# Two 16-head attentions of 32 entries each run as one sequence of 64 entries in one block

## The reference, cut to what matters

```
x = x + L0_xattn(ctx, layernorm(x), ...)        # 8 heads
x = x + L0_ffn(layernorm(x), ...)               # router picks 512 of 1536 units, up to 3 rounds
x = x + L1_xattn(layernorm(x), ctx, ctx, causal mask, w_q, w_k, w_v, w_o)   # 16 heads of 8, 120 keys
y = layernorm(x)
y = y + mla(rmsnorm(y) * g1, Wq, Wdkv, Wuk, Wuv, Wo)  # 16 heads of 8, 128 keys, causal
y = y + moe(rmsnorm(y) * g2, ...)               # 8 experts, top 2
x = x + y

# both attentions, per entry and head:
scores = q @ k.T / sqrt(8), masked;  a = softmax(scores);  out = (a @ v) @ wo
```

## Time and profile before

| | before |
|---|---|
| median of 3 runs | 1343.3 us |
| the profiled execution's own time | 1344.71 us |
| its span | 1342.9 us |
| granted TensorE clock, mean | 0.964 of full |
| busy: TensorE / VectorE / ScalarE / GpSimd | 1228.8 / 927.4 / 798.7 / 590.4 us |
| l1 pipeline | about 597 to 845 us of the span |
| mla pipeline | about 850 to 1086 us of the span |

### The profile page before, as it was taken

The page is one execution under the profiler, slowest core; times in us unless marked ns, Lnnn a source line. Parts: engine busy times, 40 slices in busy tenths (PEclk is TensorE's granted clock), DMA queues, the critical chain, the costliest instruction groups (busy, mean ns, idle before and its releaser), DMA issues. The chain is left out here.

```text
span 1342.9 us, 37984 instructions
## 1 busy us (share of the span) xinstructions
PE 1228.8 (92%) x13719; PEld 879.0 (65%) x13719; DVE 927.4 (69%) x1995; ACT 798.7 (59%) x2101; POOL 590.4 (44%) x677
## 2 busy tenths in 40 slices
PE   1799999999999995969999999599999979999996
PEld 0466666666666663437777777488888847777775
DVE  6476776776776773757989989399999956333431
ACT  0578778778778862216777777266666633333332
POOL 3587566566566555013233232543333224333343
PEclk9899999999999997988999999599999979999998
DMA  8000000000000000000000000200000000000000
GB/s 210 17 1 1 0 0 0 0 0 0 0 0 0 0 1 1 0 6 10 10 7 11 10 7 6 64 3 0 0 0 0 2 1 9 9 8 8 8 10 16
DMA packets 22740, 14.71 MB, mean 11 GB/s; under 512 B 6378, under 2 KB 21610, under 8 KB 22540
## 3 DMA queue, kind: packets, MB, share of 16 engines
q1 hardware_dynamic: 22520, 13.75, 3.9%
q10 hardware_dynamic: 148, 0.01, 0.0%
HBM read 11.66 MB, written 2.10 MB: 10 GB/s over the span
## 5 line engine op out<-in xcount | busy, mean ns | idle before, releaser
L694 POOL TENSOR_TENSOR r_norm<-ssm,mhalf 128x24 f32<-128x24 f32 x32 | 134.9, 4214 | 161.5 <-DVE ssm L599 161.5
L1938 ACT ACTIVATE moe_hid<-psum 128x512 f32<-128x512 f32 x128 | 76.4, 598 | 137.9 <-PE psum L1872 137.9
L537 ACT ACTIVATE l_probs<-psum,l_n_max 128x248 f32<-128x248 f32 x256 | 117.2, 481 | 57.5 <-DVE l_n_max L617 57.5
L2096 POOL TENSOR_TENSOR moe_acc<-moe_acc,moe_prod 128x512 f32<-128x512 f32 x64 | 81.3, 1271 | 147.8 <-DVE moe_prod L2052 147.8
L1882 PEld LDWEIGHTS psum<-w,moe_hid 128*128 128x128 f32 x1024 | 123.1, 192 | 27.0 <-issue 27.0
L2052 DVE TENSOR_TENSOR moe_prod<-psum,moe_combine 128x512 f32<-128x512 f32 x64 | 44.3, 692 | 136.2 <-PE psum L1882 136.1
L1882 PE MATMUL psum<-w,moe_hid 128*128 128x128 f32 x1024 | 123.4, 275 | 0.0
L1872 PE MATMUL psum<-moe_moe_hT,w 128*128 128x512 f32 x256 | 122.9, 608 | 0.0
L1726 POOL TENSOR_TENSOR mla_QX<-mla_qT,own_slots 128x512 f32<-128x512 f32 x32 | 33.3, 1042 | 136.0 <-ACT mla_qT L1560 136.0
L701 POOL TENSOR_TENSOR qkn<-qk,r_norm 128x1536 f32<-128x1536 f32 x32 | 88.4, 2762 | 2.5
L1726 POOL TENSOR_TENSOR l_QX<-l_qT,own_slots 128x512 f32<-128x512 f32 x32 | 33.3, 1042 | 122.3 <-ACT l_qT L1560 122.3
(11 more groups left out here) (311 smaller groups left out, 3393.2 us busy)
## 6 DMA issues: line engine op xcount, KB each, us to landing
X<-x_in SPq DMA_DIRECT2D x8, 256.0 KB, 4.9
out_dram<-moe_acc SPq DMA_DIRECT2D x32, 64.0 KB, 1.5
CT<-ctx_in SPq DMA_DIRECT2D x8, 240.0 KB, 6.1
l_cT<-ctxT_in SPq DMA_DIRECT2D x32, 60.0 KB, 1.8
w<-w_in SPq DMA_DIRECT2D x1, 1024.0 KB, 5.0
wm<-wm_in SPq DMA_DIRECT2D x1, 768.0 KB, 4.5
wp<-wp_in SPq DMA_DIRECT2D x1, 768.0 KB, 6.6
wkv<-wkv_in SPq DMA_DIRECT2D x1, 512.0 KB, 5.7
```

What stands on the lines that cost most here:

```text
L537: e = act.activation(probs[u][:, h, :], psum[:, 2 * u + h // 2, (h % 2) * K:(h % 2 + 1) * K], ACT.Exp, bias=n_max[u][:, h:h + 1], accum_ou ...
L694: pool.tensor_tensor(r_norm[:, :], ssm[:, :], mhalf[:, 0:3 * H], ALU.pow).then_inc(s["norm_inverted"], 1)
L1938: act.activation(hid[i % RING][:, :], psum[:, 2 + i % BANKS, :], ACT.Silu).then_inc(activated[i], 1)
L2096: pool.tensor_tensor(a[:, :, :], a[:, :, :], prod[e % 2][:, :, :], ALU.add).then_inc(summed[e], 1)
```

## The change

`attention16` becomes `attentions16`, which is called once. Its second block runs steps n from -2 to 65 over a sequence of 64 entries: entries 0 to 31 are l1's, entries 32 to 63 are mla's entries 0 to 31 (`is_l1`, `of_entry`, `row`). The steps inside are in the same order on each engine; a loop's body says by `l1` to which half it belongs. Steps 18 and 19 and steps 30 to 37 are among those written out.

The second attention's moments, taken of all 32 entries between the blocks before, are now taken by VectorE within the sequence: behind step 17 for entries 0 to 11 (`CHANGE = 12`), behind step 34 for entries 12 to 31. GpSimd takes the inverse roots at the end of steps 18 and 19 (12 columns each) and of steps 34, 35, 36 and 37 (10 columns each). `kT` and `probs` have room for 128 keys in both halves, of which l1 uses 120, so that l1's eight rows of 120 are no longer adjacent. SyncE's block is one: first the 32 loads of `cT`, then the expert weights.

```
-def moments(dve, stats6, mean, small, step):
+def moments(dve, stats6, mean, small, step, some=slice(0, B), base=0):
...
+def run_pair_steps(eng, body):
     for n in range(-2, 4):
         body(n, n % 2, n // 2)
     with eng.Fori(0, ROUNDS - 2) as i:
...
-    for n in range(2 * ROUNDS, 2 * ROUNDS + 2):
+    for n in range(2 * ROUNDS, 2 * ROUNDS + 4):
         body(n, n % 2, n // 2)
     with eng.Fori(0, B // 2 - 3 - ROUNDS) as i:
...
-    for n in range(B - 4, B + 2):
+    for n in range(B - 2, B + 6):
         body(n, n % 2, n // 2)
+    with eng.Fori(0, B // 2 - 4) as i:
+        body(2 * i + B + 6, 0, None, False)
+        body(2 * i + B + 7, 1, None, False)
+    for n in range(PAIR - 2, PAIR + 2):
+        body(n, n % 2, None)
...
-        probs = [sb(f"probs{i}", [P, H, K]) for i in range(2)]
+        probs = [sb(f"probs{i}", [P, H, P]) for i in range(2)]
...
+                def mla_moments(some, base):
+                    dve.wait_ge(x_stats, some.stop)
+                    moments(dve, stats6, mla_mean, small, step, some, base)
+                    dve.tensor_scalar(small[:, 0, some], small[:, 3, some], LN_EPS, None, ALU.add).then_inc(var_ready, 1)
+                    dve.tensor_scalar(small[:, 1, some], small[:, 3, some], 1.0 + RMS_EPS, RMS_EPS * LN_EPS, ALU.mult,
+                                      ALU.add).then_inc(var_ready, 1)
...
+                    if isinstance(n, int) and n == 2 * ROUNDS + 1:
+                        mla_moments(slice(0, CHANGE), 6)
+                    if isinstance(n, int) and n == B + 2:
+                        mla_moments(slice(CHANGE, B), 12)
...
+                def mla_scales(n):
+                    half = CHANGE + (B - CHANGE) // 2
+                    for at, some, ready in ((2 * ROUNDS + 2, slice(0, CHANGE), 3), (B + 2, slice(CHANGE, half), 5), (B + 4, slice(half, B), 5)):
+                        if isinstance(n, int) and n == at:
+                            pool.wait_ge(var_ready, ready)
+                            inverse_roots(pool, mla_rstd, small[:, 0, :], mhalf, some).then_inc(mla_scales_made, 1)
+                        if isinstance(n, int) and n == at + 1:
+                            inverse_roots(pool, mla_scale, small[:, 1, :], mhalf, some).then_inc(mla_scales_made, 1)
+                    if isinstance(n, int) and n in (B - 2, PAIR - 2):
+                        pool.wait_ge(mla_scales_made, 2 if n < B else 6)
...
+                def body(n, par, k, l1=None):
+                    centre(n + 1, l1)
+                    norm_output(n + 1, l1)
+                    norm_input(n + 1, l1)
                     spread_q(n + 1, 1 - par)
-                    if router and par == 0:
+                    if router and par == 0 and k is not None:
                         next_trials(k - 1)
                     later_scales(n)
+                    mla_scales(n)
```

More of the change, by code:

```diff
@@ L1312, in attention16 @@
         with nc.Block() as block:
-            if joined_from:
+            if router:
                 @block.tensor
@@ L1401, in attention16 @@
         scales_made = sem("scales_made")
+        mla_scales_made = sem("mla_scales_made")
         qkv_proj = sem("qkv_proj")
@@ L1430, in attention16, with there, is_l1, of_entry @@
         below4_made = sem("below4_made")
-        def row(T, n):
-            return T[:, entries(n), :].rearrange("p a d -> p (a d)")
+        def there(m):
+            return not isinstance(m, int) or 0 <= m < PAIR
+        def is_l1(m, l1):
+            return m < B if isinstance(m, int) else l1
+        def of_entry(T, m, l1):
+            return T[:, entries(m if is_l1(m, l1) else m - B)]
+        def row(T, m, l1):
+            return T[:, entries(m if is_l1(m, l1) else m - B), :].rearrange("p a d -> p (a d)")
+        def keys(m, l1):
+            return C if is_l1(m, l1) else P
         def round_there(k):
             return router and (not isinstance(k, int) or 0 <= k < 2 * ROUNDS)
-        def copy_input(eng, m):
+        def copy_input(eng, m, l1):
             if there(m):
@@ L1687, in body @@
                         wait(dve, totalled, k)
                     invert_sums(n - 1)
-                    if router and par == 0:
+                    if router and par == 0 and k is not None:
                         read_digit(k - 1)
                     scale_out(n - 1)
-                    max_a(n + 1, 1 - par)
+                    max_a(n + 1, 1 - par, l1)
                     if router and par == 0 and isinstance(k, int) and k == ROUNDS:
                         second_half()
-                steps(dve, body)
@@ L1710, in norm_input, with norm_output @@
                     if there(m):
+                        l1 = is_l1(m, l1)
                         wait(pool, x_centred, m + 1)
                         wait(pool, z_turned, m)
-                        pool.tensor_tensor(zn[:, :], centred[:, :], (rstd if l1 else scale)[:, entries(m)].broadcast_to([P, D]),
+                        pool.tensor_tensor(zn[:, :], centred[:, :], of_entry(rstd if l1 else mla_scale, m, l1).broadcast_to([P, D]),
                                            ALU.mult).then_inc(z_made, 1)
-                def norm_output(m):
-                    if there(m) and not l1:
+                def norm_output(m, l1):
+                    if there(m) and not is_l1(m, l1):
@@ L1757, in body @@
+                def body(n, par, k, l1=None):
+                    centre(n + 1, l1)
+                    norm_output(n + 1, l1)
+                    norm_input(n + 1, l1)
                     spread_q(n + 1, 1 - par)
-                    if router and par == 0:
+                    if router and par == 0 and k is not None:
                         next_trials(k - 1)
                     later_scales(n)
-                steps(pool, body)
-            if moe_weights:
-                @block.sync
-                def _(sp):
+                    mla_scales(n)
@@ new lines, in _, with load @@
+                run_pair_steps(pool, body)
+            @block.sync
+            def _(sp):
+                def load(m, par):
+                    wait(sp, qkv_proj, m - 1)
+                    sp.dma_start(cT[par][:, :], ctxT_in[entries(m)].rearrange("a d t -> (a d) t")).then_inc(c_loaded[par], 16)
+                load(0, 0)
+                load(1, 1)
+                with sp.Fori(0, B // 2 - 1) as i:
+                    load(2 * i + 2, 0)
+                    load(2 * i + 3, 1)
+                if moe_weights:
```

255 lines of the change are left out of this document (122 added, 133 removed).

## The result

Before 1343.91 us (median of 4 runs, 1341.84 to 1346.9), after 1333.89 us (4 runs, 1332.74 to 1335.86); ratio 0.9925, 95% interval 0.9913 to 0.9938, so 0.75% or 10.0 us less, clear of noise. The forecast was 1332.4 us, range 1328 to 1340. The profiled execution after took 1335.86 us with a span of 1333.7, so it is the slowest of its four; between the two profiled executions the span shrank by 9.2 us.

What follows compares the result with a forecast made beforehand. TensorE and VectorE were taken as full in mla's steady stretch, leaving the seam between the attentions to gain from: 22.7 us less 11.8 of costs is 10.9, from the median 1343.3 to 1332.4 us, range 1328 to 1340.

Steps and rivals of the forecast that it cites:

- seam, entries 31 to 35: Between l1 and mla: four entries' scores take 29.1 us instead of 51.8, a gain of 22.7 us.
- first moments, step 17: VectorE behind step 17: eight small rows cost 1.0 us, ends 0.3 and 1.3.
- root in step 18: GpSimd, 12 columns before entry 20's `centre`: TensorE already waits for `zn`, so its turn slips 2.3 us.
- root in step 19: GpSimd, 12 columns: 2.64 us of cover for 2.27, so cost 0; 2.3 if the cover is gone.
- wait and root in step 34: GpSimd waits for VectorE's second moments, then takes 10 columns: TensorE stands 5.0 us, ends 3.7 and 5.5.
- clock behind it: TensorE after step 35's idle: 4 to 7 us at half clock, cost 2.5 us, ends 0 and 3.5.
- roots in steps 35 to 37: GpSimd, 10 columns each: 1.96 us against 1.62 of cover, 0.34 each, 1.0 us in all.
- the clock at step 19: At step 19's start, where TensorE stands 2.3 + 0.55 us: no clock loss, 0, upper end 3.5 us.
- R1: Both stalls stay but the clock doesn't fall: net gain 13.4 us, 1330 us; chance 0.16.
- R2: Thin covers at steps 19 and 35 to 37, clock falls at both stalls: 1345 us, halfway 1339; chance 0.15.
- R3: l1's non-adjacent `probs` rows of 120 slow VectorE's shift and ScalarE's second exponential: 32 us exposed, 1364 us; chance 0.05.
- R4: Step 34's wait is not met, GpSimd being behind anyway: 0.34 us, no clock fall, net 18, 1325 us; chance 0.04.

Runs made afterwards that it cites:

- e4: Changed kernel without the in-sequence moments and roots (mean 0, scales 1 set once), a bound and no replacement: 1321.41 us, ratio 0.9836.
- e6: Changed kernel with throwaway transposes on TensorE, 24 ahead of entry 20's turn and 42 ahead of entry 36's: 1329.69 us, ratio 0.9895.
- e2: Changed kernel with the two first 12-column roots at the ends of steps 19 and 21 instead of 18 and 19: 1329.55 us, ratio 0.9892.
- e1: Changed kernel with the second moments behind VectorE's step 33 instead of step 34: 1327.82 us, ratio 0.9884.
- e3: Changed kernel with moments behind steps 18 and 33, roots at steps 19, 21 and 34 to 39 (6 or 7 columns in the last six): 1322.89 us, ratio 0.9844.
- e5: Changed kernel with CHANGE = 6 instead of 12, so first moments and roots cover 6 entries, the second 26: 1331.71 us, ratio 0.9910.

## Why the prediction was right, point by point

| term | predicted | measured in the traces |
|---|---|---|
| seam, entries 31 to 35 | 51.8 - 29.1 = 22.7 | 51.81 - 29.25 = 22.56; alone (e4) 22.0 in medians |
| first moments, step 17 | 1.0 | 0.83 (interval 7.84 against 7.01) |
| root in step 18 | 2.3, clock 0 | 4.74 = 1.97 idle (9.52 in e6 - 7.55) + 2.77 half clock |
| root in step 19 | 0 | 0.02 |
| wait and root in step 34 | 5.0 | 4.92 (e6: 11.67 - 6.75) |
| clock behind it | 2.5 | 2.47 (14.14 - 11.67) |
| roots in steps 35 to 37 | 1.0 | 0.76 over intervals of 6.75 |
| sum of costs | 11.8 | 13.7 |

- The mechanism held as it was told: the seam's gain, the queue order on GpSimd that turns a wait into TensorE's stall, the covers of 2.6 and 1.6 us, and that the clock falls at the stall of step 34. The costs of 13.7 leave 8.8 of the 9.2 us; the kernel before had itself an interval of 7.11 us before its mla entry 5, which the base of 6.75 does not count, and that is the 0.4.
- Single steps of l1 were read as 7.29 and 7.06 us, though their sum, 14.35, is not the pair of 14.51: in the loops they are 7.50 and 7.01. It did little harm. The seam's four intervals were 7.72, 7.07, 7.71 and 6.75, predicted 7.65, 7.06, 7.65 and 6.75. The root's own 2.3 was better than the table shows: over 7.29 (e2) it is 2.23.
- The 2.5 for the clock behind step 34 came true to the digit, and that is partly luck. The working, half of the stretch, would give 3.4 for the 6.8 us measured. Part of the stretch lay inside the stall, where it costs nothing, and the same stall cost 1.98 us in e2 (13.65 - 11.67).
- The term that was mis-sized is the clock at step 19, "I take 0, upper end 3.5". It measured 2.77 us in the profiled execution. The prediction gives no reason for the 0; an idle of 2.79 us was enough. That is 2.8 of the 13.7 us and more than the whole excess over 11.8, the other terms coming out 0.8 lower together; it is why the profiled execution gained 9.2 us and not 10.9. In the medians the miss is smaller, 10.0 against 10.9. That the clock's stretch varies from execution to execution (3.4 or 6.7 us at the same stall, e1) may be the cause; the four runs after, with mean clocks of 0.969, 0.969, 0.972 and 0.970, took 1335.86, 1334.59, 1332.74 and 1333.19 us, which fits but doesn't prove it.
- The root of 12 columns is 2.27 us and that of 10 is 1.96, to the digit as worked out from widths 4, 7 and 28.
- R1 (the stalls stay and the clock doesn't fall) is false in the changed kernel; e6 shows what full clock is worth there. R2 had two halves. Thin covers are false: they are there, and e2 and e3 live on them. Its other half, that the clock falls at both stalls, is what the profiled execution did. R3 is false by two rows. R4 is false: GpSimd stood 4.43 us.
- With a fall priced at 2.5 us behind step 18 as well, the sum would have been 8.4 us net, against 9.2 seen in the profiled pair.
- The Trainium skill, "TensorE: Matmul & The Clock Gate", section "HAM oscillation — how this bites in real kernels", says that idle gaps inside a kernel throttle TensorE again. The trace agrees for the stall of 4.66 us. The section speaks of gaps longer than the 2.79 us behind step 18, so it did not call for that fall; there the measurement goes beyond the page, and it decides.

## What to carry to other kernels

Joining two pipelines gives what drain, barriers, fill and cold clock cost at the seam, and it is read as the time between two equal events on either side less the steady pace. What used to stand between them must then go into the queues, and there its length counts for less than its place: the same 2.27 us root cost 4.7 us behind an even step and nothing behind an odd one, and the same moments cost 7.4 us with all that hung on them or 1.0 one step earlier. Where an in-order engine must wait for another, put the producer a step ahead of the consumer, cut the work to the width of the cover, and price a stall of a full TensorE at its length and, if the clock falls, at somewhat less than half of the cold stretch: 2.77 and 2.47 us for 6.7 and 6.8 here, since part of the stretch lies in the stall itself.

## What the runs showed of the hardware that was not expected

- A single idle of 2.79 us between dense stretches was followed by 6.7 us at half clock (2.77 us lost); one of 1.85 us was not followed by any in the one execution of e5 that was traced.
- The cold stretch behind the same stall differs: 6.7 us in the changed kernel and 3.4 in e1 with the same idle; 6.8 us behind 4.66 us of idle, but 3.4 behind 5.20 us (e5). And 6.8 us cost 2.47 us in the changed kernel and 1.98 in e2, as it began 0.9 or 2.0 us before the work came back.
- Throwaway transposes in the gap, 24 and 42 of them, kept the clock at 1.00 in the trace, with nothing else changed. In medians the changed kernel is 10.0 us below its kernel before and this one 14.4 us below its own, on another chip.
- ScalarE and VectorE took the same time for eight rows of 120 with gaps of 8 between them as for 960 adjacent elements (1041 against 1042 ns, 1141 against 1143 ns in the same stretch before).
